# Two fused layers of attention and feed-forward: new order of the steps, last norm from row sums on ScalarE

## The reference, cut to what matters

```python
x = x + masked_attention(norm(x), ctx)                 # layer 1: keys and values are the context
x = x + top2_of_8_experts(norm(x), Wr, Wg, Wu, Wd)     # layer 2: silu(x Wg) * (x Wu) Wd, weighted
x = x + topk_attention(norm(x) WqT * coef, ctx) WoT    # layer 3: only the 54 largest scores of a row
x = x + bitlinear(gelu(bitlinear(norm(x), w1)), w2)    # layer 4: rows quantised to 8 bits by their
                                                       # largest absolute value, weights to -1, 0, 1
norm(x) = (x - mean) / sqrt(var + 1e-5)
```

## Time and profile before

| | us |
|---|---|
| median of 3 runs | 428.62 |
| lowest, highest | 428.03, 429.81 |
| the profiled execution | 432.5 |
| its span in the profile | 430.8 |
| VectorE busy | 296.1 (69%) |
| TensorE busy | 358.0 (83%) |
| ScalarE busy | 178.3 (41%) |
| GpSimd busy | 51.2 (12%) |

### The profile page before, as it was taken

The page is one execution under the profiler, slowest core; times in us unless marked ns, Lnnn a source line. Parts: engine busy times, 40 slices in busy tenths (PEclk is TensorE's granted clock), DMA queues, the critical chain, the costliest instruction groups (busy, mean ns, idle before and its releaser), DMA issues. The chain is left out here.

```text
span 430.8 us, 6605 instructions
## 1 busy us (share of the span) xinstructions
PE 358.0 (83%) x2077; PEld 286.0 (66%) x2082; DVE 296.1 (69%) x760; ACT 178.3 (41%) x312; POOL 51.2 (12%) x100
## 2 busy tenths in 40 slices
...
GB/s 251 326 255 54 227 369 75 246 269 220 270 277 262 285 235 66 294 84 177 270 210 273 315 295 156 203 154 7 206 107 65 0 104 56 72 36 157 104 27 37
DMA packets 70810, 76.38 MB, mean 177 GB/s; under 512 B 5357, under 2 KB 69497, under 8 KB 70777
## 3 DMA queue, kind: packets, MB, share of 16 engines
...
...
## 5 line engine op out<-in xcount | busy, mean ns | idle before, releaser
L648 ACT ACTIVATE pT<-T 128x512 f32<-128x512 f32 (+1 forms) x64 | 32.1, 513 | 81.7 <-PE T L883 73.9
L900 PE MATMUL A<-pT,v_sb 128*128 128x128 f32 (+1 forms) x416 | 56.7, 292 | 4.1 <-DMA v_sb<-ctx 2.4
L947 PE MATMUL GU<-xgT,wg_ring 128*128 128x128 f32 x480 | 58.1, 276 | 1.5 <-DVE hid L1161 1.2
L947 PEld LDWEIGHTS GU<-xgT,wg_ring 128*128 128x128 f32 x480 | 56.6, 192 | 3.8 <-DVE hid L1161 1.4
L900 PEld LDWEIGHTS A<-pT,v_sb 128*128 128x128 f32 (+1 forms) x416 | 53.8, 206 | 7.7 <-issue 2.8
L1222 DVE MAX8 cand_h<-fold 128x8 f32<-128x801 f32 x56 | 54.5, 983 | 0.0
L869 PE MATMUL S<-k_sb,xT 128*128 128x400 f32 (+2 forms) x128 | 49.3, 523 | 0.8 <-ACT xT L633 0.8
L896 PE MATMUL A<-v_sb,pT 128*128 128x256 f32 (+1 forms) x208 | 49.1, 380 | 0.0
L869 PE MATMUL S<-k_sb,qT 128*128 128x400 f32 (+2 forms) x128 | 47.7, 515 | 1.1 <-ACT qT L707 0.9
L1234 DVE MATCH_REPLACE8 fold<-cand_h,fold 128x801 f32<-128x801 f32 x48 | 46.9, 978 | 0.0
L896 PEld LDWEIGHTS A<-v_sb,pT 128*128 128x128 f32 (+1 forms) x208 | 38.1, 190 | 6.5 <-issue 0.5
(11 more groups left out here) (154 smaller groups left out, 465.1 us busy)
## 6 DMA issues: line engine op xcount, KB each, us to landing
...
```

Source lines behind the costliest of these rows:

```text
L648: act.activation(pT[0:r, i % NPT, :, :].rearrange("p a s -> p (a s)")[:, 0:w], t_bank("pT", *key)[0:r, 0:w], ACT.Copy).then_inc(pTe_done, 1)
L900: mm = pe.matmul(A_bank[:, o * P:(o + 1) * P], v[0:r, a, o * P:(o + 1) * P], pT[0:r, j, a, :], start=m == 0 and o == 0, stop=m == NMC - 1 ...
L947: mm = pe.matmul(gu_bank(*key)[:, a * F + f * P:a * F + (f + 1) * P], wg_ring[:, w % NWG, a, k, f * P:(f + 1) * P], cols[:, k, :], start=k ...
```

## The change

Every line of ORDER differs; one of each:

```diff
-yst.0.13 down.0.14 xT.2.3 ye.0.14 xTe.2.3 yst.0.14 gat.1.0 router.2 rt1.2 gat.0.0 router.3 gat.1.1 rt1.3 egap.2 rank.1
+pvm.1.6.3 router.2 x1.6 gat.0.1 pT.1.7.1 upd.0.0 rt1.2 pT.1.7.2 gat.1.1 pvm.1.7.0 upd.1.0 upd.0.1 pTe.1.7.1 gat.2.0
```

In the new list 12 steps of TensorE that stood ahead of group 0's last `down` stand behind it: all four `pvm` of tile 6 and all four of tile 7 in layer 1, `pT.1.7.1` to `pT.1.7.3`, and one `xT` of layer 2. The clearing of the scatter array (`zero`, a DMA of 1920 KB) and the load of `w1` come within the first dozen DMAs. Group 1's routing stands between the score chunks of tile 0 in layer 3. Step by step of the code:

```diff
+WHOLE = tuple(range(NT - 2))
 # gpsimd
+ elif op == "nmax":  pool.wait_ge(maxH_done, n("maxH", t, 0)); pool.tensor_scalar(nmax3[:, t:t + 1], cand_h[:, t % 2, 0:1], -1.0, ...)
+ elif op == "xdeq":  pool.wait_ge(xmx_done, n("xmx", t)); pool.wait_ge(wdeq_done, 1)
+                     pool.tensor_tensor(xdeq[:, t:t + 1], xmx[:, t:t + 1], wdeq_q[:, :], ALU.mult)
+ elif op == "gdeq":  pool.wait_ge(gmx_done, n("gmx", t)); pool.wait_ge(wqb_done, 2); pool.tensor_tensor(gdeq[:, t:t + 1], ...)
+ elif op == "va4":   pool.wait_ge(sq4_done, n("sq4", t))
+                     pool.tensor_scalar(var4[:, t:t + 1], square4[:, t:t + 1], 1.0 / D, D * D * EPS, ALU.mult, ALU.add)
 # scalar
+ act.wait_ge(x_in[0], 16)            # ahead of its first DMAs, mask and Wr
+ elif op == "cent":  act.wait_ge(x3_done, n("x3", t)); if t >= 2: act.wait_ge(q4_done, n("q4", t - 2))
+                     act.activation(xn4[:, t % 2, :], x_res[:, t, :], ACT.Identity, bias=sum4[:, t:t + 1], scale=-float(D))
+ elif op == "sq4":   act.wait_ge(x3_done, n("x3", t))
+                     act.activation(squares[:, :], x_res[:, t, :], ACT.Square, bias=sum4[:, t:t + 1], scale=-float(D),
+                                    accum_out=square4[:, t:t + 1])
 # vector
+ wqb: if which == 1: dve.tensor_scalar(wdeq_q[:, :], wdeq[:, 0:1], 1.0 / 127.0, None, ALU.mult)
- nmax, st4, ag4, va4, cent, xdeq, gdeq
  x3:  dve.scalar_tensor_tensor(out=x_res[:, t, :], in0=O_bank[:, 0:D], scalar=r3[:, t:t + 1],
-                               in1=x_res[:, t, :], op0=ALU.mult, op1=ALU.add)
+                               in1=x_res[:, t, :], op0=ALU.mult, op1=ALU.add, accum_out=sum4[:, t:t + 1])
  xscl: scalar 127.0 -> -127.0
  gabs: for t in WHOLE one reduction over all 1024 columns, after both halves of gelu; else one for each half as before
  gmx:  for t in WHOLE without the joining tensor_tensor
```

More of the change, by code:

```diff
@@ L143 @@
-dn.1 s3e.7.2 repH.4.3 pTe.3.3.3 repH.5.0 maxH.4.4 s3.6.0 s3.6.2 fin.1 ginv.0 ag4.2 repL.4.1 store.1 gmul.0 va4.2
-repH.4.4 h4T.0 cent.2 s3e.6.0 rs4.2 s3e.6.2 s3.7.3 maxH.4.5 pvm.3.3.3 gdeq.0 h4e.0 xabs.2 maxH.5.1 aTe.3 maxL.4.2 dn.0
-fin.0 nmax.4 s3.6.3 repH.5.1 store.0 s3e.7.3 wo.3 xmx.2 repH.4.5 s3e.6.3 repL.5.0 xinv.2 maxH.5.2 repL.4.2 maxL.5.1
-maxL.4.3 repH.5.2 xscl.2 maxH.4.6 xmul.2 q4.2 maxH.5.3 exp3.4 nmax.5 merge.4 q4e.2 xdeq.2 repH.5.3 up.2.0 x3.3
-gelu.2.0 up.2.1 thr.4 maxH.5.4 gelu.2.1 cut.4.0 repH.5.4 pT.3.4.0 pTe.3.4.0 repL.5.1 pairL.6 exp3.5 pT.3.4.1 pT.3.4.2
@@ L148 @@
-pvm.3.4.0 s3.7.1 ldv.3.4.2 gabs.2.0 pTe.3.4.1 maxH.5.5 pTe.3.4.2 gabs.2.1 st4.3 ldv.3.4.3 maxL.5.2 ag4.3 repH.5.5
-repL.5.2 s3e.7.1 pairH.6 pvm.3.4.1 pT.3.4.3 maxL.5.3 gmx.2 s3.7.0 maxH.5.6 ginv.2 maxH.6.0 rc3.4 gdeq.2 ldv.3.5.0
-repH.6.0 pTe.3.4.3 pvm.3.4.2 merge.5 ldv.3.5.1 va4.3 gmul.2 h4T.2 maxH.6.1 cent.3 pvm.3.4.3 aTe.4 h4e.2 maxL.6.0 thr.5
-repH.6.1 repL.6.0 ldv.3.5.3 s3e.7.0 nmax.6 maxH.6.2 cut.5.0 repH.6.2 maxL.6.1 pT.3.5.0 pairH.7 xabs.3 pairL.7 maxH.6.3
-pTe.3.5.0 pvm.3.5.0 ldv.3.5.2 wo.4 pT.3.5.1 repL.6.1 pT.3.5.2 repH.6.3 pTe.3.5.1 pTe.3.5.2 pvm.3.5.1 exp3.6 pT.3.5.3
@@ L158 @@
-q4e.3 up.3.1 rc3.5 xdeq.3 merge.7 x3.5 thr.7 gelu.3.1 st4.4 wo.6 cut.7.0 pT.3.7.0 up.3.0 ag4.4 cut.7.1 st4.5 pTe.3.7.0
-pT.3.7.1 gelu.3.0 va4.4 cent.4 rc3.6 rs4.4 xabs.4 xmx.4 pvm.3.7.0 ag4.5 pTe.3.7.1 ldv.3.7.2 xinv.4 cut.7.2 xscl.4
-va4.5 gabs.3.1 pT.3.7.2 xmul.4 xdeq.4 rs4.5 gabs.3.0 q4.4 pTe.3.7.2 x3.6 pvm.3.7.1 q4e.4 gmx.3 ginv.3 cent.5 gmul.3
-up.4.0 st4.6 up.4.1 xabs.5 ag4.6 va4.6 cent.6 gelu.4.0 h4T.3 xmx.5 cut.7.3 rs4.6 xabs.6 pT.3.7.3 gelu.4.1 xdeq.5
-gabs.4.0 pvm.3.7.2 xinv.5 xmx.6 xscl.5 xinv.6 xscl.6 h4e.3 gabs.4.1 gmx.4 xmul.5 xmul.6 pTe.3.7.3 q4.5 dn.3 q4e.5
@@ L163 @@
[L163 to L167 removed]
+ldx.0 stats.1.0 ldx.2 ldk.1.0.3 ldx.3 ldk.1.0.1 ldk.1.0.0 ldk.1.0.2 ldx.1 zero wload.1 aggr.1.0 var.1.0 rstd.1.0
@@ new lines @@
+gabs.0.0 repH.5.1 s3e.6.3 repH.4.5 xinv.2 xdeq.2 s3.7.1 va4.3 s3.7.2 rs4.3 gmx.0 maxL.5.1 ginv.0 maxH.4.6 repL.5.1
+merge.4 cent.3 maxH.5.2 gmul.0 thr.4 xabs.3 s3e.7.1 nmax.5 h4T.0 xscl.2 s3.7.0 s3e.7.2 cut.4.0 h4e.0 gdeq.0 dn.0
+xmul.2 fin.0 pT.3.4.0 pTe.3.4.0 s3e.7.0 up.1.0 repH.5.2 pairH.6 store.0 pvm.3.4.0 xmx.3 gelu.1.0 up.1.1 pT.3.4.1
+maxH.5.3 q4.2 pairL.6 xinv.3 repH.5.3 gelu.1.1 maxL.5.2 pTe.3.4.1 ldv.3.4.2 q4e.2 pT.3.4.2 pvm.3.4.1 maxH.6.0 maxH.5.4
+gabs.1.0 up.2.1 repH.6.0 up.2.0 repH.5.4 xscl.3 maxH.6.1 pT.3.4.3 pTe.3.4.2 pTe.3.4.3 gelu.2.1 xmul.3 gelu.2.0
```

284 lines of the change are left out of this document (152 added, 132 removed).

## The result

| | before | after |
|---|---|---|
| median of 4 runs each, side by side (us) | 429.22 | 417.97 |
| lowest, highest | 428.03, 430.16 | 415.21, 423.42 |
| the profiled execution | 432.5 | 416.91 |
| its span | 430.8 | 415.2 |
| mean granted clock of TensorE | 0.931 | 0.971 |

The ratio of the times is 0.9717, with a 95% interval of 0.967 to 0.9764: the change makes the kernel about 2.8% faster, 11 to 12 us. The ratio leaves out the execution of 423.42 us, which lies more than 1.5% above the fastest one and counts as slow. The forecast was 412.5 us with a range of 405 to 423.5; the 418.0 lies inside it, 1 us above the stretch (407 to 417) that the prediction called the forecast.

The account below looks back on a forecast made before the run. TensorE bounds until about 164 us, VectorE from 200 to 400, with a hollow between and a three-engine tail. Terms -12.5 + 2.2 - 1.4 - 3.6 + 1.9 - 2.7 = -16.1 from 432.5 give 416.4, less 3.9 is 412.5 us; range 405 to 423.5.

Parts of the forecast that it names:

- Step 1: Before group 0's last `down`: twelve TensorE steps leave a stretch that TensorE bounds, -12.5 us.
- Step 2: Start and group 0's expert pass: weights get less time to land (+1.5), early loads delay the start (+0.7), together +2.2 us.
- Step 3: Last `down` of group 0 to first fold: work and wait lie side by side, 26 us instead of 27.4, -1.4.
- Rival B: Hollow before the first fold: TensorE's clock still falls, +7.5 us, 420 us in all; chance 0.09.
- Step 4: First fold to `merge.7`: VectorE saves 4.6 us of small steps, less 1.0 for steps now ahead of `merge.7`, -3.6.
- Step 5: Group 1's expert pass: fewer VectorE steps between first and last `mul`, so late weights stop VectorE, +1.9 us, bounds 0 to 8.
- rival D: Last norm: VectorE waits for ScalarE at `xabs`; at 2.3 us a tile 431 us, slower than before; chance 0.06.
- Step 6: Last norm in the tail: from `x3.7` to its `xmx` 2.35 us instead of 2.27; earlier it hides under VectorE's searches.
- Step 7: Tail from `merge.7` to the span's end: ScalarE binds, `x3.7` at 12.6, end at 28.8 instead of 31.5, -2.7 us.
- the median of the runs stands 3.9 us below it, and I carry that over: Whole kernel: 3.9 us taken off the 416.4 summed for a profiled execution, giving 412.5 us.
- Rival A: Both expert passes: DMA binds them, +4.5 and +6.1 us over the sum, 423 us; chance 0.14.
- Rival E: Around group 0's end and first fold: moved steps only move the wait, gain 5 instead of 13.9 us, 421.5; chance 0.08.

Follow-up runs that it names:

- order_only: The changed kernel's new order of all steps, with the last norm's code as in before; 426.2 us against 429.0 of before, ratio 0.9954.
- norm_only: The order of before with only the last norm's code changed; 433.0 us against 429.0 of before, ratio 1.0091.
- cent_dve: The changed kernel with the last norm's centring on VectorE instead of ScalarE; 419.4 us against 430.8 of before.
- tail_moved: The changed kernel with `gmul.3`, `gmul.4`, the centring and `h4e.6` on VectorE, other places for `pT.7.3`, `pvm`, `aTe.7`; 418.4 us against 431.3 of before.
- tail_filled: tail_moved with later `w1` load and sums, seven dummy matmuls ahead of `wo.6`, zeros issued ahead of `ldv.1.2.2`; 415.9 us, ratio 0.9678 to before.
- front_only: New order up to tile 0's first searches in layer 3, then the order of before, with the norm of before; 436.1 us against 429.0, ratio 1.019.

## Why the prediction was right, and what missed

The direction and the mechanism held: the hollow is filled, the fold comes 11 us earlier and VectorE has less to do. For the profiled execution the sum said 416.4, and that of the change took 416.9, but so near a hit is luck: the first trace of before was the longer one of its kernel and the first of the change the shorter one. The median missed by 5.5 us. Step by step, with two traces of each kernel:

- **Step 1, twelve TensorE steps leave, -12.5.** Right. Start to start, `pvm` ahead of the last `down` falls from 45.1 to 33.8 us, `pT` and `xT` by 1.7 together: -13.0.
- **Step 2, +2.2.** It came to 4.0, nearly twice that: the last `down` ends at 154.7 and 155.3, not 153.9, so on the mean of both traces 9.0 earlier than before, not 10.3. Idle time of TensorE up to there rose by 1.4 to 1.8, and score steps and expert tiles stretched by some 2.2 although shown as busy. At the start the first transposition is 2.2 us earlier, which the sum didn't have, and 1.4 and 2.1 us of waiting for keys (one of 1.4 in the second trace) give it back.
- **Step 3, 26 us from `down` to fold.** Right: 25.7 and 26.9, with the clock at 1.00. Rival B did not come.
- **Step 4, VectorE -3.6.** Right, and in its parts: work fell from 202.6 to 199.1, 3.5. In the traces the statistics, centrings and one-column steps of the old list, with the joins and the merged `gabs`, make 4.6, and the steps of tiles 4 and 5 that are new ahead of `merge.7` (`xabs.4`, `x3.5` and short ones) 1.0 to 1.1. What the forecast didn't give is the price of the norm in the new order: that has six tiles' statistics and centrings ahead of `merge.7` where the old one has four. By order_only the order adds 4.0 and the norm then takes 7.5 away; in the old order it takes 3.9 (norm_only). So the 2.9 for keeping `cent` and `st4` on VectorE, and the 3.6 expected of order_only, were counted for too few tiles. The page of the Trainium skill that spoke against the move, "ScalarE: Activation LUTs", section "Rules for kernel authors", has VectorE as the faster engine for such steps. The traces agree on the price: the centring takes VectorE 0.34 us and ScalarE 0.50. What the rule would cost here no run shows alone: with only the centring back on VectorE the time is the same, with the whole old norm there it is 8 us longer.
- **Step 5, less cover, +1.9.** Waits rose from 5.2 and 2.8 to 6.4 and 7.2, by 2.8 on the mean. At `mul`, which is what the term was for, they rose from 2.2 and 1.4 to 3.4 in both traces, +1.6, some 2.5 of the 3.4 at the first two. The other large rise is at `xabs`, from nothing to 1.3 and 1.8: rival D's wait, under its bound of 2, but without a term in the sum.
- **Step 6.** From `x3.7` to `xmx` 2.29 (2.35 forecast).
- **Step 7, the tail.** 29.4 instead of 28.8, but in other parts: `x3.7` stands 13.9 after `merge.7` instead of 12.6, and what follows it takes 15.5 instead of 16.2. The forecast laid the gain to the order and 0.1 us of loss to the norm. order_only shows it the other way round: with the old norm the new order's tail is 31.2, with `x3.7` at 14.0 and 17.2 behind it, so the order gives 0.9 up to `x3.7` and the norm 1.7 behind it. (A table load of 1.28 us on ScalarE stands at 399.49 in before, and none behind `merge.7` in after; order_only has none there either, so it isn't what shortens the tail.) ScalarE was named as the bound. cent_dve and tail_moved speak against that; some 0.5 us belongs to the clock by tail_filled, in one trace and with its filler's own delay in it. What binds was not separated further; with the filling TensorE is busy 14.8 of the 16 us from 384 to 400, so its own work is the next candidate.
- **The largest miss** is "the median of the runs stands 3.9 us below it, and I carry that over". It took the place of one execution in the scatter of before for an offset that the changed kernel would share. The first trace of before stood 3.9 above its median, the two of the change 1.1 below and 0.6 above theirs. A sum of differences from a high execution also counts what that execution had too much, such as its 2.4 us of waits. This offset is 3.9 of the 5.5 us; most of the rest is step 2. By the mean of two traces each the change gains 13.4 us (9.0 + 1.35 + 0.65 + 2.45), by the medians 11.2 and 11.8; the sum said 16.1.

Rival A (DMA binds both passes) came in part: 310 GB/s at a share of 1.01 from 120 to 140 us of after (the earlier trace rows had 303 at 0.99), and step 2 came to 4.0 us, where A had 6.7. VectorE's 3.4 us before `mul` are over the 3 us that the prediction named as A's sign, but before already had 2.2 and 1.4 there. Rival E did not come: the fold is 11.2 and 9.5 us earlier, although group 1's routing stands between tile 0's score steps. A kin of it, which the prediction had not weighed, decides front_only: group 1's rows are no earlier, and only a list that fills the time with searches and scores of other tiles keeps what the early fold brings.
